# Four narrow graph passes: TensorE's share of the columns from 18 to 16 of 28, twelve unpaced gathers

## The reference

```python
x = layernorm(x + segment_sum(tanh(x[src] * edge_weight), dst))        # layer 0
x = layernorm(x + edge_softmax_layer(x, edge_attr_16, src, dst))      # layer 1
h = segment_max(x[src] * edge_weight1, dst)                           # layer 2
x = layernorm(x + h @ W.T + b)
agg = segment_sum(x[src], dst)                                        # layer 3, twice
h = relu((1 + eps) * x + agg @ wa + ba) @ wb + bb
```

## Time and profile before

| | before |
|---|---|
| median of three runs | 8206.96 us |
| profiled execution, its own time | 8196.03 us |
| its span | 8194.2 us |
| granted TensorE clock, mean over the span | 0.959 |
| busy: PE, DVE, POOL, ACT | 87%, 85%, 65%, 19% |
| pass 0 | from 89 us to about 1272 us |
| attention | from there to about 4674 us |
| passes 1, 2, 3 | from about 4683, 5844 and 7010 us to 5826, 6987 and 8150 us |

### The profile page before, as it was taken

How to read it: one execution, slowest core, us unless ns; L and a number is a source line. 1 busy time by engine, 2 the same in 40 slices (tenths; PEclk the granted TensorE clock), 3 DMA queues, 4 the chain that set the end, 5 groups by cost and what they waited for, 6 DMA issues and landing times.

```text
span 8194.2 us, 205237 instructions
## 1 busy us (share of the span) xinstructions
PE 7100.0 (87%) x77871; PEld 6660.7 (81%) x77871; DVE 6989.1 (85%) x12224; ACT 1570.8 (19%) x3861; POOL 5336.9 (65%) x4570
## 2 busy tenths in 40 slices
PE   5999985888888988888887099999499997799994
PEld 5999975777777777777776099999499997799994
DVE  7999976999999999999999488888488886688884
ACT  0000002444444444444443200000000000000000
POOL 3555557888888888888886655555455555455554
PEclk9999998999999999999999599999799998899997
DMA  2222213555555455455554211111111111111110
GB/s 88 87 83 87 87 48 91 152 155 155 152 155 156 152 156 154 152 156 155 152 155 145 77 48 46 47 48 46 29 48 48 48 48 32 42 48 47 47 48 21
DMA packets 738221, 757.27 MB, mean 92 GB/s; under 512 B 153760, under 2 KB 698336, under 8 KB 738112
## 3 DMA queue, kind: packets, MB, share of 16 engines
q1 hardware_dynamic: 592640, 667.34, 24.7%
q0 software_dynamic: 140528, 86.77, 6.7%
q10 hardware_dynamic: 5008, 2.59, 0.1%
HBM read 239.80 MB, written 519.73 MB: 93 GB/s over the span
## 4 chain that ended last, share of the span: by engine, by line
PE 41%; DVE 30%; issue 23%; POOL 4%; DMA 1%; DVEq 1%; ACT 0%; ACTq 0%; POOLq 0%; SPq 0%; another core or an unknown queue 0%
PE ps L798 41%; DVE amax_room L1206 6%; DVE spare L1211 4%; DVE flat L1233 3%; DVE msg L1111 2%; DVE stt L928 2%; POOL got L451 2%; DVE flat L928 2%; DVE run L1132 1%; DVE spare L1215 1%; DVE raw L928 1%; DVE wide_buf L928 1%; DVE flat L1090 1%; DVE junk L1138 1%; POOL wide_buf L451 1%
## 5 line engine op out<-in xcount | busy, mean ns | idle before, releaser
L451 POOL DMA_INDIRECT msg<-feat,cidx x1680 | 1686.0, 1004 | 1580.9 <-PE ps L798 1172.2
L798 PE MATMUL ps<-parts,wide_buf 128*128 128x160 bf16 x30240 | 2123.2, 233 | 291.1 <-DVE wide_buf L1090 279.7
L798 PEld LDWEIGHTS ps<-parts,wide_buf 128*128 128x128 bf16 x30240 | 2100.2, 98 | 303.8 <-issue 283.7
L451 POOL DMA_INDIRECT hsrc<-feat,aidx x1568 | 1897.0, 1210 | 457.8 <-issue 327.8
L798 PE MATMUL ps<-parts,flat 128*128 128x160 bf16 x30240 | 2113.3, 233 | 25.7 <-DVE flat L1090 21.1
L798 PEld LDWEIGHTS ps<-parts,flat 128*128 128x128 bf16 x30240 | 2093.6, 98 | 33.1 <-DVE flat L1090 25.1
L845 PEld LDWEIGHTS ps<-wsb,zT 102*128 102x128 f32 x9408 | 1464.1, 190 | 222.9 <-ACT zT L684 201.2
L845 PE MATMUL ps<-wsb,zT 102*128 102x192 f32 (+1 forms) x9408 | 1543.3, 313 | 101.9 <-ACT zT L684 101.2
L1111 DVE TENSOR_REDUCE msg<-raw 128x288 f32<-128x2880 f32 x224 | 1130.4, 5046 | 7.8
L928 DVE TENSOR_TENSOR raw<-ps,amask 128x960 f32<-128x960 f32 x448 | 737.9, 1657 | 463.4 <-PE ps L798 351.0
L451 POOL DMA_INDIRECT msg<-in_x,cidx x560 | 561.3, 1002 | 553.5 <-PE ps L798 310.0
(11 more groups left out here) (218 smaller groups left out, 4681.3 us busy)
## 6 DMA issues: line engine op xcount, KB each, us to landing
state_tab<-flat SPq DMA_DIRECT2D x784, 512.0 KB
raw<-quot_tab SPq DMA_DIRECT2D x224, 576.0 KB
run_tab<-run SPq DMA_DIRECT2D x224, 224.0 KB
top_tab<-spare SPq DMA_DIRECT2D x392, 128.0 KB
msg<-feat,cidx POOLq DMA_INDIRECT x1680
hsrc<-feat,aidx POOLq DMA_INDIRECT x1568
efs<-in_ef SPq DMA_DIRECT2D x392, 34.0 KB
msg<-in_x,cidx POOLq DMA_INDIRECT x560
```

What stands on the lines that cost most here:

```text
L451: return pool.indirect_dma_start(dest, None, table, rows_at(idx))
L798: last = nc.tensor.matmul(block.rearrange("p (q c) -> p q c", c=D), hot[s][:, m, t * P:(t + 1) * P], parts[:, m * Q:(m + 1) * Q, part, :], ...
```

## The change

R becomes 16, so A becomes 12. TensorE makes 240 matmuls for a group in place of 270, and the twelve `pick` signals come at every 20th. DVE now waits for the fifth before the own columns. The ten shared columns fill three banks and a third of the fourth, so the multiplication of the shared columns becomes two instructions, of nine columns (128x1440) and of one (128x160). POOL issues a group's twelve gathers with no wait between them; the waits for the index copy and for the use of the slot stay. Two tiles that had been sized by R get a fixed size, ROOM = 7168 elements in place of 8064.

```diff
-R = 18
+R = 16
+ROOM = 4 * DC * DD
+RW = OWN + (R - OWN) // CB * CB
-        wide_buf = sb("wide_buf", [P, 7 * R * P // 2])
+        wide_buf = sb("wide_buf", [P, ROOM])
-        flat = sb("flat", [P, 7 * R * P // 2])
+        flat = sb("flat", [P, ROOM])
                         for u in range(A):
-                            if u:
-                                pool.wait_ge(q["pick"][s], (done + j) * A + u)
-                                pool.sem_inc(s_pool, 1)
                             gather(msg[:, s, u, :], table, cidx[:, s, u:u + 1]).then_inc(q["got"][s], 16)
                     dve.wait_ge(q["pick"][s], (done + j + 1) * A)
-                    tt(picked_rows(OWN, R), shared.rearrange("p b (r c) -> p b r c", c=D), mask_rows(OWN, R),
-                       ALU.mult).then_inc(s_share, 1)
+                    last = tt(picked_rows(OWN, RW), shared[:, 0:(RW - OWN) // CB].rearrange("p b (r c) -> p b r c", c=D), mask_rows(OWN, RW),
+                              ALU.mult)
+                    if RW < R:
+                        last = tt(picked[:, RW:R], shared[:, (RW - OWN) // CB, 0:(R - RW) * QW].rearrange("p (r q c) -> p r q c", q=Q, c=D),
+                                  amask[:, RW:R].unsqueeze(3).to_broadcast([P, R - RW, Q, D]), ALU.mult)
+                    last.then_inc(s_share, 1)
```

More of the change, by code:

```diff
@@ L59 @@
 CONT, BOTH, CONT_NEG, BOTH_NEG = range(4)
-assert MB * (Q - 1) < NB <= MB * Q and CB * QW <= 512 and OWN == 2 * CB and R - OWN == 4 * CB and K % DW == 0
+assert MB * (Q - 1) < NB <= MB * Q and CB * QW <= 512 and OWN == 2 * CB and R - OWN <= 4 * CB and K % DW == 0
 FP = mybir.dt.float32
```

## The result

| | before | after |
|---|---|---|
| median of four runs, us | 8205.75 (8202.72 to 8208.66) | 10761.74 (10758.5 to 10766.01) |
| ratio | 1 | 1.3115 [1.3093, 1.3138] |
| span of the profiled execution | 8194.2 | 10759.0 |
| one group in pass 0 / in pass 1 | 19.8 / 18.7 us | 32.5 / 30.5 us |

The account below looks back on a forecast made before the run. TensorE was taken to bound passes 1 to 3 and pass 0's last six groups, DVE pass 0's first 50. Gains of 350 + 61 + 12 + 5 = 428 us gave a 7777 us median, range 7755 to 7850.

Parts of the forecast that it names:

- POOL's paragraph: Gathers on POOL: twelve in 16.1 us a group, 0.5 below TensorE; in pass 0 thirteen in 17.3 against DVE's 18.57.
- So the removed waits bring nothing by themselves; they only let twelve fit: POOL's gathers: no gain of their own from removing the waits, only room for twelve gathers in 16.66 us.
- The early start costs nothing: POOL's gathers for two groups later: 16.1 us plus 2.3 to land, wanted after 33 us.
- Nothing in the form of a matmul changes, so the spacing stays.: TensorE's matmuls: each still costs its spacing, 69.4 ns, so 30 fewer save 2.08 us a group.
- the gathers hold DVE: Rival: seven DVE operations a group each wait half a gather, +3.3 us; +110 us in all, 8317 us; chance 3%.
- TensorE, 2.08 us a group: TensorE in passes 1 to 3: 30 matmuls fewer, 18.74 to 16.66 us a group, 350 us in all.
- a gain of 428 us: Whole kernel: sum of 350 us in passes 1 to 3, 61 and 12 in pass 0, 5 at ends of passes.
- DVE, -1.22 us a group: DVE's own work: sum -0.56, multiplications -0.27, one-hots -0.37, mask -0.02 us; between -0.85 and -1.27.
- forecast 18.57: Pass 0, first 50 groups, DVE's chain: 19.79 falls by 1.22 to 18.57 us a group, 61 us in all.
- POOL, 16.1 us of gathers and issue: POOL's twelve gathers a group: 15.0 us bare, some 0.9 beside one-hots, 0.2 for irregular stalls.
- 14 us to spare: POOL's use of the slot: gathers need 16.1 us and 2.3 to land, DVE wants them after 33 us.
- noise (0.2 us a group): POOL's gather time: 0.2 us a group allowed for irregular stalls that all engines show now and then.

Follow-up runs that it names:

- set 2: Changed kernel with fixed row indices, wide matmuls with waits, wide matmuls without, half the rows: 7756.6, 7710.28, 7708.66, 7756.45 us; kernel before 8179.81.
- wide matmuls: Changed kernel with 8 matmuls a column for 15, same streamed columns: without waits 7708.66 or 9512.56 us, with waits 7710.28 or 8192.43.
- set 1: Changed kernel with waits back 8550.76 us, with plain DMAs 8518.59; 17 columns with waits 8306.31; kernel before without waits 10330.19, unedited 8211.9.

## Why the prediction was wrong, point by point

- **The step that failed is POOL's paragraph**: "So the removed waits bring nothing by themselves; they only let twelve fit", and "The early start costs nothing". It counted gathers as a load on POOL alone. The waits for `pick` spread ten gathers over 18.7 us; without them the same gathers come in one run and hold TensorE. This was shown on the kernel before alone (10330 us), on the changed one with the waits back (8551), and with another kind of DMA in place of the gathers (16.6 us a group). It failed only where TensorE starves: in set 2 the waits were worth nothing, as forecast (7710.28 us with them, 7708.66 without, both with wide matmuls), and two kernels with narrow matmuls and unpaced gathers, which fetched other or fewer rows, took 7757 and 7756 us against a forecast of 7777. The prediction did not know of two such conditions; the one trace of before shows only the starved one, in the event from 7242.48 us.
- **"Nothing in the form of a matmul changes, so the spacing stays."** The form did stay, but the spacing depends on POOL: 69.4 ns when fed, some 480 ns while starved, 137 ns for the next 5 us. No rival named TensorE as the victim. The nearest, "the gathers hold DVE", named the wrong engine: the one-hots of 16 columns took 747 to 768 ns where TensorE starved and where it did not, and those of 18 columns 815 to 821, as before.
- **TensorE, 2.08 us a group.** Right where nothing starves: 16.6 us a group (set 1 with plain DMAs, set 2 in pass 1). With the waits kept, where it starves, the removed matmuls are worth less than nothing: +0.5 and +1.1 us for the 17th and 16th column. The split, priced at a gain of 428 us, is with the waits kept a loss of 339. (A slip of no weight: 8206.96 - 428 is 7779, not 7777.)
- **DVE, -1.22 us a group.** Right: in the rows above 0.747, 4.480 and 1.658 us, each within 1%, and 0.314 for the small multiplication priced at 0.33. Pass 0 in set 2 ran at 18.6, forecast 18.57.
- **POOL, 16.1 us of gathers and issue.** Too high and of no importance: the run takes 15.2 us in the starved kernel, and in set 2 (351.5 us busy and 362 x 0.30 of issue in 500 us) 15.3 a group, beside a TensorE busy all the time.
- **The serial circle was missed too.** I had 14 us to spare between a gather's start and its use. That holds for the data. But the next run starts only when DVE has multiplied the last weights, which waits for TensorE, which waits for this run's end. So run (15.2 us) and recovery (15.5) follow one another and don't overlap, once a group.
- **The clue was there.** The earlier trace rows show TensorE one group after another without a gap; the few "issue" gaps in the trace of before were put down as noise (0.2 us a group) where I should have asked what ran just ahead of them.

One reading of the cause lies near and is not shown. The Trainium skill, "Runtime: NRT & Kernel Launch", section "Instruction fetch mechanics", says that an engine's instructions are themselves fetched by DMA in blocks, mostly hidden. A store used up by number and a supply in steps would fit a fetch that the indirect form delays. The profiles speak against it: of the kind "instruction" they list 42 DMA packets with 0.51 MB in the whole execution of the changed kernel, just as many in the sequential gathers of set 2, which did not starve, and none from 6000 to 7000 us, where 33 groups starve. A supply of one to five matmuls at a time doesn't look like blocks either. Unless the list is incomplete, it is another part of TensorE's supply that is held up.

**What stays open.** Which resource the indirect form takes from TensorE's supply: rows and addresses are excluded, duration on POOL (0.95 against 0.58 us) is not. Why one set of six was free of it, on a chip number that was starved in another set; this sets the limit of every "shown" above, which holds for the starved condition. Whether the unmodified changed kernel would take some 7756 us in such a set: it was not run there, only two kernels that equal it in pass 0. And why 18 columns are the best with the waits: (gathers x 1.25 us) + (matmuls - gathers x 3.8) / 38 gives 18.6, 19.4 and 20.1 us for 18, 17 and 16 columns, against 18.7, 19.2 and 20.3, but two of its numbers are fitted to three points.

## What to carry to other kernels

A wait that "costs nothing" can be the pacing that another engine lives on: before removing it, ask what its instructions do when they come in one run. Where TensorE works through short matmuls, keep indirect DMAs of GpSimd apart (here runs of at most four cost 1.5%, runs of five 16.7%), or use plain DMAs where the rows follow one another. An idle gap with no releaser in a trace of before is a row to be explained: look at what every other engine did in the 10 us ahead of it.

## What the runs showed of the hardware

- Twelve indirect DMAs 0.30 us apart held TensorE to 28 matmuls in 13.4 us; plain DMAs issued by the same engine, 575 ns each and with next to no gap, did not, with 7232 matmuls in 500 us.
- Half the rows of each gather changed nothing (10801 against 10776 us). On TensorE's side it goes by instructions: starved, it got 2.1 narrow or 2.0 wide matmuls a microsecond, and about half as many matmuls for the same work put off the first gap from 3.8 to about 10.6 us.
- The same kernel took 7709 us in one set of runs and 9513 in another, while the kernel before moved only from 8180 to 8201. A quiet kernel as the comparison does not tell in which condition a set is; a starved control does.
- TensorE came back from such a pause at half clock for about 5 us: 37 matmuls of 137 ns, then 70.
